# The LayerNorm root of a fused Mamba and MoE kernel: its seed from integer operations on VectorE, with three Newton steps on GpSimd, in place of a logarithm and an exponential on ScalarE

## The reference

```python
xn = layernorm(x)
x_ssm, x_gate = split(xn @ in_w.T + in_b)
x_conv = silu(causal_conv4(x_ssm) + conv_b)
B, C = split(x_conv @ bc_w.T + bc_b)          # 16 states each
dt = softplus(x_conv @ dt_w.T + dt_b)
h = h * exp(dt * A) + dt * B * x_conv         # over 512 steps, 16 states
y = (sum_n h * C + x_conv * D) * silu(x_gate)
z = y @ out_w.T + out_b + xn
mamba = (z - mean(z)) * rsqrt(var(z) + 1e-5) * ln_g + ln_b
moe = xn + sum over 2 of 8 experts of w_e * (silu(xn @ we1 + be1) @ we2 + be2)
out = x + mamba + moe
```

## Time and profile before

| what | value |
|---|---|
| median of three runs | 915.27 us (911.18 to 916.78) |
| the profiled execution | 913.16 us, its span 911.0 us |
| mean granted TensorE clock | 0.963 of full speed |
| TensorE busy | 778.3 us, 85% |
| VectorE busy | 787.3 us, 86% |
| ScalarE busy | 662.7 us, 73% |
| GpSimd busy | 602.0 us, 66% |
| table loads at L824 | 7, 1283 ns each |

### The profile page before, as it was taken

The page is one execution under the profiler, slowest core; times in us unless marked ns, Lnnn a source line. Parts: engine busy times, 40 slices in busy tenths (PEclk is TensorE's granted clock), DMA queues, the critical chain, the costliest instruction groups (busy, mean ns, idle before and its releaser), DMA issues.

```text
span 911.0 us, 14381 instructions
## 1 busy us (share of the span) xinstructions
PE 778.3 (85%) x4533; PEld 625.8 (69%) x4533; DVE 787.3 (86%) x774; ACT 662.7 (73%) x1134; POOL 602.0 (66%) x384
## 2 busy tenths in 40 slices
PE   2994959988998999899998899989998998899932
PEld 1661747867776778677876787678767776779821
DVE  7917948899989988998899889989899989989993
ACT  1433678878689868986897779796897689869910
POOL 3580425767577758775777757885688487758851
PEclk9996879999999999999999999999999999999975
DMA  9949547667576867697668866785688576987541
GB/s 297 382 171 304 198 142 235 198 195 240 189 258 213 241 207 237 206 274 246 208 208 253 269 204 201 225 285 155 216 229 276 183 259 204 255 270 220 158 91 23
DMA packets 81928, 201.02 MB, mean 221 GB/s; under 512 B 7936, under 2 KB 41216, under 8 KB 81728
## 3 DMA queue, kind: packets, MB, share of 16 engines
q1 hardware_dynamic: 61424, 171.46, 54.7%
q0 software_dynamic: 19168, 26.59, 15.0%
q10 hardware_dynamic: 1264, 2.05, 0.7%
HBM read 174.38 MB, written 26.61 MB: 221 GB/s over the span
## 4 chain that ended last, share of the span: by engine, by line
DVE 30%; PE 25%; DMA 13%; ACT 11%; issue 9%; POOL 4%; DVEq 0%; POOLq 0%; SPq 0%; ACTq 0%
DVE ps_drive L954 11%; PE ps_up L1248 10%; DMA out<-yo,sid 7%; DVE ring L961 6%; DVE ps_drive L947 6%; PE ps_yx L1262 5%; PE ps_fr L1179 4%; DMA out<-xtok 3%; ACT L805 3%; ACT da L778 3%; DMA bc_scratch<-sp 2%; PE ps_fr L1204 2%; DVE xx L928 1%; POOL y L598 1%; PE ps_up L1242 1%
## 5 line engine op out<-in xcount | busy, mean ns | idle before, releaser
L598 POOL TENSOR_TENSOR y<-y,ring 128x1024 f32<-128x1024 f32 x126 | 322.9, 2563 | 61.9 <-ACT y L769 50.7
L954 DVE TENSOR_TENSOR_SCAN ps_drive<-da,ps_drive 128x1024 f32<-128x1024 f32 x128 | 293.7, 2295 | 28.1 <-ACT da L778 24.4
L1248 PEld LDWEIGHTS ps_up<-xgt,w1s 128*128 128x128 f32 x2272 | 278.9, 193 | 17.7 <-issue 9.6
L1248 PE MATMUL ps_up<-xgt,w1s 128*128 128x128 f32 x2272 | 278.7, 276 | 0.0
L1262 PE MATMUL ps_yx<-w,ht 128*128 x1136 | 268.3, 379 | 0.0
L1262 PEld LDWEIGHTS ps_yx<-w,ht 128*128 128x128 f32 x1136 | 204.7, 190 | 28.1 <-issue 5.0
L587 POOL DMA_INDIRECT out<-yo,sid x71 | 119.7, 1685 | 121.0 <-ACT yo L820 49.6
L805 ACT ACT_TABLE_LOAD x143 | 183.5, 1283 | 2.5
L947 DVE TENSOR_TENSOR ps_drive<-ps_u,rep 128x1024 f32<-128x1024 f32 x128 | 157.4, 1229 | 27.2 <-DMA rep<-bc_scratch 18.4
L778 ACT ACTIVATE da<-gd,col 128x511 f32<-128x511 f32 x256 | 168.4, 710 | 0.0
L961 DVE TENSOR_TENSOR ring<-ps_drive,rep 128x1024 f32<-128x1024 f32 x128 | 156.6, 1223 | 3.9
(11 more groups left out here) (172 smaller groups left out, 711.2 us busy)
## 6 DMA issues: line engine op xcount, KB each, us to landing
w1s<-in_we SPq DMA_DIRECT2D x71, 1024.0 KB, 7.5
rep<-bc_scratch SPq DMA_DIRECT2D x128, 512.0 KB, 4.8
w<-in_we SPq DMA_DIRECT2D x8, 1024.0 KB, 12.0
w<-in_x SPq DMA_DIRECT2D x8, 512.0 KB, 10.9
xn_scratch<-da SPq DMA_DIRECT2D x8, 512.0 KB, 7.4
xnt_scratch<-xx SPq DMA_DIRECT2D x8, 512.0 KB, 6.0
out<-w POOLq DMA_DIRECT2D x8, 512.0 KB, 6.4
xx<-xnt_scratch SPq DMA_DIRECT2D x8, 512.0 KB, 3.3
```

The costliest lines, as they stand in the source:

```text
L598: pool.tensor_tensor(y[:, :, :], y[:, :, :], ring[:, g % RING, :, :], ALU.add).then_inc(s_sum, 1)
L954: dve.tensor_tensor_scan(states, da[:, g % DECAYS, :, :].rearrange("p k l -> p (k l)"), states, 0.0, ALU.mult, ALU.add).then_inc(s_scanned, 1)
L1248: mm = pe.matmul(bank[:, c * P:(c + 1) * P], w1s[:, q, k, at:at + P], xgt[:, k, :], start=False, stop=(c == 3 and k == KD - 1))
```

## The change

The logarithm and the exponential leave ScalarE, with the table load that the logarithm needed. VectorE now adds the epsilon, shifts the bits of the variance right by one as an integer, and forms 0x5F3759DF minus that, which read as a float is a rough root. The three instructions stand at k = 0, 1 and 2 of step 2. Since this seed is rougher, GpSimd takes three Newton steps in place of one: the first in step 2 behind `add_state` r = 1, the second in step 3 behind the scatter, the third with the two closing operations behind `add_state` r = 1 of step 3.

```diff
@@ -480,6 +480,8 @@
         CT = KD * (TAPS - 1)
+        NEWTON = 3
+        NN = 4 * NEWTON + 2
...
@@ -603,25 +605,25 @@
-                def add_eps(b):
-                    var = mv[:, :, 1]
-                    pool.wait_ge(s_ln_meanvar, (b + 1) * TB)
-                    pool.tensor_scalar(var, var, EPS, None, ALU.add).then_inc(s_ln_eps, 1)
-
-                def newton(b):
-
-                    pool.wait_ge(s_ln_seed, b + 1)
-                    pool.wait_ge(s_ln_eps, b + 1)
+                def newton(b, n):
+
+                    done = b * NN + 4 * n
+                    if n == 0:
+                        pool.wait_ge(s_ln_seed, b + 1)
+                    else:
+                        pool.wait_ge(s_ln_newton, done)
                     pool.tensor_tensor(rt_t[:, :], rstd[:, :], rstd[:, :], ALU.mult).then_inc(s_ln_newton, 1)
-                    pool.wait_ge(s_ln_newton, b * 6 + 1)
+                    pool.wait_ge(s_ln_newton, done + 1)
                     pool.tensor_tensor(rt_t[:, :], rt_t[:, :], mv[:, :, 1], ALU.mult).then_inc(s_ln_newton, 1)
-                    pool.wait_ge(s_ln_newton, b * 6 + 2)
+                    pool.wait_ge(s_ln_newton, done + 2)
                     pool.tensor_scalar(rt_t[:, :], rt_t[:, :], -0.5, 1.5, ALU.mult, ALU.add).then_inc(s_ln_newton, 1)
-                    pool.wait_ge(s_ln_newton, b * 6 + 3)
+                    pool.wait_ge(s_ln_newton, done + 3)
                     pool.tensor_tensor(rstd[:, :], rt_t[:, :], rstd[:, :], ALU.mult).then_inc(s_ln_newton, 1)
-                    pool.wait_ge(s_ln_newton, b * 6 + 4)
+
+                def shift_of(b):
+                    pool.wait_ge(s_ln_newton, b * NN + 4 * NEWTON)
                     pool.tensor_tensor(rt_t[:, :], mv[:, :, 0], rstd[:, :], ALU.mult).then_inc(s_ln_newton, 1)
-                    pool.wait_ge(s_ln_newton, b * 6 + 5)
+                    pool.wait_ge(s_ln_newton, b * NN + 4 * NEWTON + 1)
                     pool.tensor_scalar(rt_t[:, :], rt_t[:, :], -1.0, None, ALU.mult).then_inc(s_ln_newton, 1)
...
@@ -642,12 +644,15 @@
                         add_state(b, i, 0)
                     if not (last and i == STEPS - 1):
                         scatter(s, b, i)
-                    if i == 2 and prev is not None:
-                        add_eps(prev)
                     if i == 3 and prev is not None:
-                        newton(prev)
+                        newton(prev, 1)
                     if i < IN and not (last and i == IN - 1):
                         add_state(b, i, 1)
+                    if i == 2 and prev is not None:
+                        newton(prev, 0)
+                    if i == 3 and prev is not None:
+                        newton(prev, 2)
+                        shift_of(prev)
...
@@ -819,16 +824,8 @@
-                def seed_root(b):
-                    act.wait_ge(s_ln_eps, b + 1)
-                    act.activation(rt_l[:, :], mv[:, :, 1], ACT.Ln).then_inc(s_ln_log, 1)
-
-                def seed_exp(b):
-                    act.wait_ge(s_ln_log, b + 1)
-                    act.activation(rstd[:, :], rt_l[:, :], ACT.Exp, scale=-0.5).then_inc(s_ln_seed, 1)
-
                 def normalise(b):
-                    act.wait_ge(s_ln_newton, b * 6 + 6)
+                    act.wait_ge(s_ln_newton, (b + 1) * NN)
...
@@ -857,11 +854,7 @@
-                    if i == 3 and b > 0:
-                        seed_root(b - 1)
                     table_of(ACT.Exp)
-                    if i == 3 and b > 0:
-                        seed_exp(b - 1)
                     if s + 2 < MT:
                         copy_x(s + 2)
...
@@ -982,10 +975,26 @@
                     if b > 0:
-                        dve.wait_ge(s_ln_newton, b * 6)
+                        dve.wait_ge(s_ln_newton, b * NN)
                     dve.wait_ge(s_ln_stats, counted)
                     for j in range(TB):
                         dve.bn_aggr(mv[:, j, :], stat[:, j, :]).then_inc(s_ln_meanvar, 1)
+
+                def add_eps(b):
+                    dve.wait_ge(s_ln_meanvar, (b + 1) * TB)
+                    dve.tensor_scalar(mv[:, :, 1], mv[:, :, 1], EPS, None, ALU.add).then_inc(s_ln_eps, 1)
+
+                def shift_bits(b):
+                    dve.wait_ge(s_ln_eps, b + 1)
+                    dve.tensor_single_scalar(rt_i[:, :], mv[:, :, 1].bitcast(I32), 1,
+                                             ALU.logical_shift_right).then_inc(s_ln_shifted, 1)
+
+                def seed_root(b):
+                    dve.wait_ge(s_ln_shifted, b + 1)
+                    if b > 0:
+                        dve.wait_ge(s_ln_normed, b * TB)
+                    dve.tensor_scalar(rstd[:, :].bitcast(I32), rt_i[:, :], -1.0, float(0x5F3759DF),
+                                      ALU.mult, ALU.add).then_inc(s_ln_seed, 1)
...
@@ -1003,6 +1012,8 @@
+                    if i == 2 and k < 3 and last >= 0:
+                        (add_eps, shift_bits, seed_root)[k](last)
                     if i in (2, 3) and k >= 5 and b < B - 1:
                         tap(b + 1, i - 2, k - 4)
...
@@ -1151,7 +1162,7 @@
                 dve.wait_ge(s_xtok, B * 16)
-                dve.wait_ge(s_ln_newton, (B - 1) * 6)
+                dve.wait_ge(s_ln_newton, (B - 1) * NN)
```

2 lines of the change are left out of this document (1 added, 1 removed).

## The result

The changed kernel took **931.96 us** (median of 6 runs, 925.28 to 939.36); the kernel before took 912.70 us beside it (6 runs, 911.18 to 916.78). The ratio is 1.0187, with a 95% interval of 1.0148 to 1.0226. The forecast was 916.5 us, within 909 to 923: the kernel became slower, and the range did not hold the time. The profiled execution took 925.28 us, span 923.5 us, 12.5 us more than before.

What follows compares the result with a forecast made beforehand. VectorE was taken to set the time from the end of step 2 to step 6, ScalarE and TensorE the rest. 913.16 + 0 + 1.0 + 0 + 1.8 = 916.0 us, as a median 916.5, range 909.0 to 923.0 us.

Steps and rivals of the forecast that it cites:

- ScalarE's 11.2 us are worth 0 on the path: Step 3: removed load, logarithm and exponential save 1.60 us a batch, all waited away at step 6's B and C store.
- GpSimd's longer stream costs 0: Steps 2 and 3: seven more small GpSimd operations, 2.0 us a batch, 13.8 us in all, add nothing to the path.
- the earlier `weigh`: Step 3: the `weigh` GpSimd waits for comes 1.6 us sooner, leaving 1.2 us of cover for its added operations.
- The seeds cost 1.0 us, between 0.5 and 3.4: Step 2, batch 7: three small VectorE operations, the second held about 0.5 us by a running `add_state`; 1.0 us on the path.
- The cover in batches 1 to 6: Step 2: VectorE's wait for B and C rows, 2.46 us in batch 3, hides the seeds; without it 6 us more.
- The rival with the tap behind `add_state`: Step 3: first tap falls behind `add_state` r = 0, up to 1.9 us in six batches: 927.6 us, chance 0.06.
- Taps and Newton steps alternate, 1.8 us: Step 3: second Newton step overlaps the last two taps, 0.3 us a batch, 1.8 us over batches 1 to 6.
- From the profiled execution to a median: Whole kernel: sum of 916.0 us for the profiled execution, 2.1 us below the runs' median, became 916.5 us.
- TensorE's wait behind the removed load: Step 3: TensorE's wait for the copy, 1.87 us, was to shrink to about 0.3 us.
- the first tap of step 3 takes over 1 us: Step 3: a sign that the prediction is wrong on the slower side.
- VectorE's stream in batch 7 grows by more than 1 us: Batch 7: a sign that the prediction is wrong on the slower side.
- the store waits: Step 6: ScalarE's waits for the B and C store were to grow from 8.9 to 18.5 us.

Runs made afterwards that it cites:

- the version through PSUM: Changed kernel with epsilon back on GpSimd, shift and subtraction through a PSUM corner and moved behind the r = 0 multiply by C: 912.37 us, 0.9992 to the kernel before.
- the cliff: Section on the kernel before with ScalarE's seed kept and three Newton steps on GpSimd in step 3: 949.23 us, ratio 1.0380.

## Why the prediction was wrong

- **ScalarE's 11.2 us are worth 0 on the path**: nearly right for the kernel before (at most 4.0 us, ratio 0.9983). As a reason it was incomplete: with the longer GpSimd stream the same work costs 17 us (912.37 against 929.29 us).
- **GpSimd's longer stream costs 0**: right in the version through PSUM (ratio 0.9992), and for the reason given ("without the earlier `weigh` it would be 1.1 us a batch, 7.7 us"), but the other bound was mis-sized: without the earlier `weigh` it is some 17 us. How it comes to so much is open (the cliff, above).
- **The seeds cost 1.0 us, between 0.5 and 3.4**: this is the step that failed. It priced a hold only behind an `add_state` that is already running, for batch 7, and took GpSimd's issue of gathers and scatters as harmless. The seeds took 38.3 us, 6.1 us in batch 7 alone, where the batch grew by 4.2 us. GpSimd's gathers and scatters stood in the timeline of before; what was missing was that an operation that starts late in such an issue is kept for the sum behind as well.
- **The cover in batches 1 to 6** ("if the cover were gone it would cost 6 us more"): the cover held in all six for the seeds, but it was used up (VectorE's waits for B and C rows fell from 18.4 to 4.4 us), and what came behind, the held taps, had none: 9.5 us in batches 3 and 5.
- **The rival with the tap behind `add_state`** (927.6 us, chance 0.06) is what happened, at another place. It was priced at step 3, with `add_state` r = 0, by a margin of 0.5 us, and "`add_state` r = 1 comes after the taps" was held against it. The taps met r = 1, in step 2, because the epsilon's operation had gone from between scatter and sum, which the order of the change shows and the prediction read only as a shorter stream. It was priced at 1.9 us in each of six batches and is 4.7 us in each batch it meets, in two batches of one profile and three of the other. That its total, 927.6 us, lies close to the measured 931.96 is luck.
- **Taps and Newton steps alternate, 1.8 us**: in step 3 nothing of that size is seen; undisturbed pairs take 1.53 us. In batch 3 the pair there took 3.49 us, behind the sum again; in both profiles of the changed kernel this happened, of batches 1 to 6, in just those whose pair of step 2 was held.
- **From the profiled execution to a median**: 916.0 us lies 2.1 us lower than a median would by the prediction's own figures, and it added 0.5. This decides nothing here; the six runs of the kernel before have their median at 912.70 us.
- Of the signs listed, TensorE's wait behind the removed load came out as said (0.26 us in batches 1 to 6, for 1.87), and so did the 7 table loads; ScalarE was 8.9 us less busy, not 11. The others: "the first tap of step 3 takes over 1 us" did not come (0.73 us), "VectorE's stream in batch 7 grows by more than 1 us" did, by 4.2 us, and the store waits did not grow in the change, since VectorE was late; they did where VectorE was on time (12.5 to 12.8 us).

The trace of the kernel before already held the case that the prediction took as harmless. In batch 2 a tap started 0.85 us into a gather's issue, 0.17 us ahead of the sum, and took 3.08 us; this is more than the 2.65 us that the prediction had as the worst:

```profile
356.35 3.08 DVE L928 SCALAR_TENSOR_TENSOR xx<-xs,col,xx 128x512 f32<-128x512 f32 x1 [0.55 <-ACT xx L706]
```

```profile
355.50 1.01 POOL L578 DMA_INDIRECT xg<-xn_scratch,gid  x1 [0.17 <-issue]
356.52 2.35 POOL L598 TENSOR_TENSOR y<-y,ring 128x1024 f32<-128x1024 f32 x1
```

## What to carry to other kernels

Before a small operation is put on VectorE, look at what GpSimd has in hand at its place, the issue of indirect transfers included, and at what comes right behind that on GpSimd: the hold lasts until that has ended. When a small operation is taken away from between a GpSimd transfer and a large GpSimd operation, look at which VectorE operation now starts late in the issue. Read merged rows one by one there: of a pair only the second was held. The cure that these runs show is the place: right behind the end of the large operation the seeds took 0.16 to 0.17 us. Whether a side in PSUM would have done the same at the old place was not tried.

## What the runs showed of the hardware

- VectorE's 128 by 4 operation with both sides in SBUF, started 0.41 to 0.51 us after a gather's issue on GpSimd, took 2.9 to 3.0 us, to the end of the 128 by 1024 sum behind the gather (43 of 43). Ten that started 0.92 us after it took 0.16 us, and the sum there began 0.1 us later than usual. The Trainium skill ("SBUF — State Buffer", Who interferes with whom) has the shared pair of ports held by the one that starts first for the whole instruction; the trace agrees where the sum is already running (the tap 0.54 us into a sum in step 3 of batch 3 took 2.71 us), and shows in addition that a wait which begins late in GpSimd's issue of a transfer lasts through its next instruction.
- What follows the issue decides. Taps that started 0.76 to 1.04 us into a scatter's issue took 3.5 to 3.8 us with the 128 by 1024 sum right behind it; with a 128 by 4 operation there, the epsilon or a Newton step, taps that started up to 1.41 us into the issue took 0.72 to 0.80 us, all 154 of them.
- Two streams that meet once a batch give steps and not a slope: the two profiled executions of the changed kernel, spans 923.5 and 929.2 us, held the taps in two batches and in three.
